# A quarter of a layer's value projection moved into later blocks, a zero fill issued one stage earlier, and idle matmuls in the norm stages

## What is computed

```python
x = x + tanh(g_xattn[0]) * L0_xattn(layernorm(x), ctx, ctx, ...)   # 8x8 heads of width 2
x = x + tanh(g_ffn[0])   * L0_ffn(layernorm(x), ...)               # top-2 of 8 experts, capacity 256
x = x + tanh(g_xattn[1]) * L1_xattn(layernorm(x), ctx, ctx, ...)   # 16 heads of width 64
x = x + tanh(g_ffn[1])   * L1_ffn(layernorm(x), ...)               # int8 matmul
x = x + tanh(g_xattn[2]) * L2_xattn(...)                           # 16 heads of width 8, biased
x = x + tanh(g_ffn[2])   * L2_ffn(...)                             # dense mix of 15 experts
x = x + tanh(g_xattn[3]) * L3_xattn(...)                           # 16 heads of width 8, masked
x = x + tanh(g_ffn[3])   * L3_ffn(...)                             # ternary weights
```

## Time and profile before

| | us |
|---|---|
| median of three runs | 1626.92 |
| the profiled execution, its own time | 1622.71 |
| span of its trace | 1620.9 |
| PE busy | 1379.8 (85%) |
| DVE busy | 1062.6 (66%) |
| ACT busy | 778.8 (48%) |
| POOL busy | 649.0 (40%) |
| mean granted clock of TensorE | 0.895 of 2.4 GHz |

### The profile page before, as it was taken

How to read it: one execution, slowest core, us unless ns; L and a number is a source line. 1 busy time by engine, 2 the same in 40 slices (tenths; PEclk the granted TensorE clock), 3 DMA queues, 4 the chain that set the end, 5 groups by cost and what they waited for, 6 DMA issues and landing times. The chain is left out here.

```text
span 1620.9 us, 29634 instructions
## 1 busy us (share of the span) xinstructions
PE 1379.8 (85%) x10158; PEld 739.9 (46%) x10166; DVE 1062.6 (66%) x3273; ACT 778.8 (48%) x1105; POOL 649.0 (40%) x505
## 2 busy tenths in 40 slices
PE   5999965749999999998339999997999489999981
PEld 3444453615666666666313333333677223333431
DVE  4887744166676666764688777763556787777725
ACT  3777721336665665654113555554433125555550
POOL 4666613514676666777632112200600432332000
PEclk7999976958999999999557999998899769999995
DMA  4566623535342233400054334401200133223001
GB/s 140 193 238 233 241 88 118 157 123 214 143 151 90 101 143 145 155 1 1 17 118 78 75 73 110 86 2 45 48 1 1 25 49 54 38 42 59 13 2 29
DMA packets 87990, 147.57 MB, mean 91 GB/s; under 512 B 15875, under 2 KB 61086, under 8 KB 84261
## 3 DMA queue, kind: packets, MB, share of 16 engines
q1 hardware_dynamic: 84510, 116.94, 25.9%
q10 hardware_dynamic: 1824, 25.17, 4.0%
q0 software_dynamic: 1520, 3.68, 0.9%
HBM read 93.66 MB, written 45.11 MB: 86 GB/s over the span
## 5 line engine op out<-in xcount | busy, mean ns | idle before, releaser
L1834 DVE CUSTOM_DVE_ANT_0 a_junk<-a_psM,a_madd 128x512 bf16<-128x512 f32 x512 | 332.2, 683 | 92.1 <-issue 89.4
L1780 ACT ACTIVATE a_probs<-a_psE 128x1024 f32<-128x1024 f32 x256 | 262.0, 1023 | 214.8 <-PE a_psE L1669 213.9
L2235 DVE TENSOR_REDUCE a_mx<-a_psM 128x1 f32<-128x512 f32 x236 | 148.1, 668 | 124.2 <-PE a_psM L2060 124.2
L1669 PE MATMUL a_psE<-a_maddT,res_identb 64*128 64x512 bf16 x1024 | 221.8, 388 | 2.1
L1646 PE MATMUL a_psM<-narrow_k_op,narrow_q_op 57*128 57x512 bf16 (+1 forms) x512 | 153.0, 415 | 42.1 <-DMA narrow_q_op<-a_y_parts 20.3
L2197 ACT ACTIVATE a_probs<-a_psE 128x1024 f32<-128x1024 f32 x128 | 130.8, 1024 | 85.3 <-PE a_psE L2082 82.0
L190 POOL TENSOR_SCALAR res_xn<-res_X,res_mv,n_rstd 128x128 f32<-128x128 f32 x32 | 26.8, 847 | 352.9 <-DVE n_rstd L176 352.9
L1680 PE MATMUL a_psO<-a_probs,narrow_values 128*32 128x256 f32 x2048 | 164.0, 394 | 2.5 <-ACT a_probs L1780 1.1
L2030 POOL TENSOR_TENSOR a_half_sum<-a_probs 128x1024 f32<-128x1024 f32 x64 | 150.8, 2356 | 32.9 <-ACT a_probs L2197 32.7
L2078 PE MATMUL a_psE<-a_qT,a_kT 64*128 64x256 f32 x1024 | 133.4, 380 | 0.0
L2094 PE MATMUL a_psO<-a_probs,a_values 128*64 128x256 f32 x1024 | 124.6, 385 | 0.8 <-ACT a_o_raw L2181 0.8
(11 more groups left out here) (334 smaller groups left out, 2528.4 us busy)
## 6 DMA issues: line engine op xcount, KB each, us to landing
wide_k<-a_k_stage SPq DMA_DIRECT2D x32, 512.0 KB, 3.2
wide_v<-a_v_stage SPq DMA_DIRECT2D x32, 512.0 KB, 4.3
a_k_part<-wide_k SPq DMA_DIRECT2D x64, 256.0 KB, 3.4
a_kT<-wide_k ACTq DMA_DIRECT2D x6, 2048.0 KB, 8.2
a_values<-wide_v ACTq DMA_DIRECT2D x6, 2048.0 KB, 8.6
keys<-a_parts SPq DMA_DIRECT2D x96, 64.0 KB, 2.0
narrow_q_op<-a_y_parts SPq DMA_DIRECT2D x192, 32.0 KB
narrow_k_op<-keys SPq DMA_DIRECT2D x30, 192.0 KB
```

Source lines behind the costliest of these rows:

```text
L1669: return pe.matmul(psE[s % 2][:, j, :, :], res.identb[group, :], maddT[r][group, s % 2 * 2:s % 2 * 2 + 2, :], start=False, stop=last, skip ...
L1780: act.activation(probs[:, head:head + 2, k:k + 2, :], psE[s % 2][:], ACT.Exp).then_inc(exped, 1)
L1834: dve.tensor_tensor_reduce(junk[j][:], psM[j][:], madd[r][:, t, :], 1.0, -3.0e38, ALU.add, ALU.max, mx[r][:, max_place(h, t):max_place(h, ...
L2235: dve.tensor_reduce(mx[r][:, at:at + 1], max_bank(2 * p + t, j, first), AX.X, ALU.max).then_inc(max_read, 1)
```

## The change

1. `v_stage`, the stores and the loop of wide values in the first layer's attention go from four key tiles to three (KT - 1). The fourth tile's two matmuls per chunk are made by a new class `LateValues`: chunks 0 to 3 in the router's block (`queue_up`), chunks 4 to 7 in the experts' block. `w1v` and `ctxT` stay in SBUF until then. Each chunk has a stage buffer of its own; two PSUM banks are shared.
2. The zero fill of `y_dram` is issued in `project_out`, from a tile cleared by DVE, and its end is awaited there.
3. `norm_phase`, where transposed, starts its PE program with 36 matmuls of bf16 128x128 by 128x128 into a bank that nobody reads.

```diff
+IDLE_MATMULS = 36
+def keep_busy(pe, res, bank, n):
+    for _ in range(n):
+        pe.matmul(bank, res.identb[:], res.onesb[:], start=True, stop=True)
@@ norm_phase
             def _(pe):
                 if transposed:
+                    keep_busy(pe, res, psI[:], IDLE_MATMULS)
                     for c in range(NCHUNK):
@@ attend_layer0
-        n_wide = W_PAIRS + KT * VC
+        n_wide = W_PAIRS + (KT - 1) * VC
...
-                    for k in range(KT):
+                    for k in range(KT - 1):
                         sp.wait_ge(wide_out, n_wide * n + W_PAIRS + VC * (k + 1))
                         sp.dma_start(res.wide_v[one, :, k].rearrange("o p c -> (o p) c"), v_stage[k][:]).then_inc(wv_stored[k], 16)
...
-                    for k in range(2, KT):
+                    for k in range(2, KT - 1):
                         wide_values(i, k, first)
@@ project_out
+    zeros = ph.sb("zeros", [P, 2 * D])
...
-            sp.wait_ge(zeroed, 1)
+            sp.wait_ge(zeroed, 2)
             sp.dma_start(bo[0:1, :], io[bo_name].unsqueeze(0)).then_inc(w_in, 16)
             for sem, count in res.stores:
                 sp.wait_ge(sem, count * (B * S2 // CHUNK))
+            sp.dma_start(res.y_dram[0:2 * NTILE * P].rearrange("(p n k) d -> p n (k d)", p=P, k=2),
+                         zeros[:].unsqueeze(1).to_broadcast([P, NTILE, 2 * D])).then_inc(y_zeroed, 16)
             constants.sync(sp, io, constants_in)
+            sp.wait_ge(y_zeroed, 16)
...
+            dve.memset(zeros[:], 0.0).then_inc(zeroed, 1)
             dve.memset(bo[:], 0.0).then_inc(zeroed, 1)
@@ new class
+class LateValues:
+    def __init__(self, ph, res, chunks, banks=None):
+        self.stage = [ph.sb(f"late{j}", [P, WIDE_V]) for j in range(len(chunks))]
+        self.ps = banks or [ph.ps(f"psV{i}", [P, CHUNK]) for i in range(2)]
+    def tensor(self, pe):
+        for j, n in enumerate(self.chunks):
+            keys = self.res.ctxT[:, 2 * n:2 * n + 2].rearrange("d t n c -> d (t n c)")[:, (KT - 1) * P:KT * P]
+            for c in range(VC):
+                m = VC * j + c
+                if m >= 2:
+                    pe.wait_ge(self.out, m - 1)
+                pe.matmul(self.ps[m % 2][:], keys, self.res.w1v[:, c * CHUNK:(c + 1) * CHUNK], start=True, stop=True).then_inc(self.made, 1)
+    def scalar(self, act):
+                act.wait_ge(self.made, m + 1)
+                act.copy(self.stage[j][:, c * CHUNK:(c + 1) * CHUNK], self.ps[m % 2][:]).then_inc(self.out, 1)
+    def sync(self, sp):
+        for j, n in enumerate(self.chunks):
+            sp.wait_ge(self.out, VC * (j + 1))
+            sp.dma_start(self.res.wide_v[n, :, KT - 1], self.stage[j][:]).then_inc(self.stored, 16)
+    def finish(self, sp):
+        sp.wait_ge(self.stored, 16 * len(self.chunks))
@@ queue_up
+    late = LateValues(ph, res, range(B // 2))
             sp.dma_start(xn_dram.rearrange("(t p) d -> p t d", p=P), res.xn[:]).then_inc(xn_out, 16)
-            sp.wait_ge(zero_made, 1)
-            sp.dma_start(y_dram[0:2 * N_TOKENS]..., zeros...).then_inc(y_zeroed, 16)
+            late.sync(sp)
             sp.wait_ge(xn_out, 16)
-            sp.wait_ge(y_zeroed, 16)
+            late.finish(sp)
...
             router.scalar(act)
+            late.scalar(act)
             act.wait_ge(router.hot, 2)
             act.copy(chose[:], onehot[:]).then_inc(ones_cast, 1)
...
+            late.tensor(pe)
             pe.wait_ge(ones_cast, 2)
...
-            pool.memset(zeros[:], 0.0).then_inc(zero_made, 1)
@@ queued_experts
+        late = LateValues(ph, res, range(B // 2, B), banks)
                 load(0, 0)
                 load(1, 1)
+                late.sync(sp)
                 for e in range(2, E):
                     sp.wait_ge(made, e - 1)
                     load(e, e % 2)
+                late.finish(sp)
...
+                late.tensor(pe)
                 turn(0)
...
             def _(act):
+                late.scalar(act)
                 for e in range(E):
```

More of the change, by code:

```diff
@@ L160, in norm_phase @@
         psT = [ph.ps(f"psT{i}", [P, CHUNK]) for i in range(2)]
+        psI = ph.ps("psI", [P, P])
         var_done, std_done, newton = ph.sem("var_done"), ph.sem("std_done"), ph.sem("newton")
@@ L271, in attend_layer0 @@
     k_stage = [outer.sb(f"k_stage{i}", [P, 2, S2]) for i in range(4)]
-    v_stage = [outer.sb(f"v_stage{i}", [P, WIDE_V]) for i in range(KT)]
+    v_stage = [outer.sb(f"v_stage{i}", [P, WIDE_V]) for i in range(KT - 1)]
     parts = [outer.sb(f"parts{i}", [P, 3, CHUNK], BF16) for i in range(2)]
@@ L305, in attend_layer0 @@
         wide_made, wide_out = ph.sem("wide_made"), ph.sem("wide_out")
-        wk_stored, wv_stored = [ph.sem(f"wk_stored{i}") for i in range(4)], [ph.sem(f"wv_stored{i}") for i in range(KT)]
+        wk_stored, wv_stored = [ph.sem(f"wk_stored{i}") for i in range(4)], [ph.sem(f"wv_stored{i}") for i in range(KT - 1)]
         minus_done = ph.sem("minus_done")
@@ L778, in vector @@
         dve.wait_ge(self.hot, top_k)
+class LateValues:
+    def __init__(self, ph, res, chunks, banks=None):
+        self.res, self.chunks = res, chunks
+        self.stage = [ph.sb(f"late{j}", [P, WIDE_V]) for j in range(len(chunks))]
+        self.ps = banks or [ph.ps(f"psV{i}", [P, CHUNK]) for i in range(2)]
+        self.made, self.out, self.stored = ph.sem("late_made"), ph.sem("late_out"), ph.sem("late_stored")
+    def tensor(self, pe):
[7 more added lines that the diff above has]
+    def scalar(self, act):
+        for j in range(len(self.chunks)):
+            for c in range(VC):
+                m = VC * j + c
+                act.wait_ge(self.made, m + 1)
[6 more added lines that the diff above has]
+        sp.wait_ge(self.stored, 16 * len(self.chunks))
 def layer0_experts(nc, io, res):
@@ L975, in queued_experts @@
         psH = [ph.ps(f"psH{i}", [P, C]) for i in range(4)]
-        psY = [ph.ps(f"psY{i}", [P, ROW_HALVES, D]) for i in range(2)]
+        banks = [ph.ps(f"psY{i}", [P, CHUNK]) for i in range(2)]
+        psY = [bank[:, 0:ROW_HALVES * D].rearrange("p (r d) -> p r d", d=D) for bank in banks]
         w_in, x_in = [ph.sem(f"w_in{i}") for i in range(2)], [ph.sem(f"x_in{e}") for e in range(E)]
@@ L1040, in _ @@
                         pe.matmul(psH[k][:], w1[b][:, k * P:(k + 1) * P], xgT[b][:], start=True, stop=True).then_inc(hidden, 1)
+                    if e == 0:
+                        pe.wait_ge(late.out, VC * len(late.chunks))
                     if e >= 2:
@@ L1080, in _ @@
                     dve.wait_ge(made, e + 1)
-                    dve.tensor_copy(y[:, e], psY[e % 2][:]).then_inc(y_copied, 1)
+                    dve.tensor_copy(y[:, e], psY[e % 2]).then_inc(y_copied, 1)
                 for c in range(NCHUNK):
@@ L2566, in build @@
                 layer0_attention(nc, io, res)
-            Phase.clear_used(nc)
-            layer0_experts(nc, io, res)
+                Phase.clear_used(nc)
+                layer0_experts(nc, io, res)
             norm_phase(nc, io, res, "n2")
```

14 lines of the change are left out of this document (6 added, 8 removed).

## The result

The changed kernel takes 1600.67 us (median of four runs, 1599.92 to 1602.52) against 1626.84 us before (four runs, 1626.61 to 1629.39): ratio 0.9838, 95% interval 0.9824 to 0.9851. That is 26.2 us less, where the prediction had 13.4 less and a range that ended at 1606.0. The sign was right; time and range were wrong. The profiled execution took 1600.32 us for a span of 1598.6; its mean granted clock is 0.915 of full speed against 0.895 before.

What follows compares the result with a forecast made beforehand. PE was taken to bound the first layer's attention. Terms -13.3 + 2.5 + 1.3 + 0 + 0.7 - 0.6 - 4.0 = -13.4 us took the median 1626.92 to 1613.5 us, range 1606 to 1620.5.

Steps and rivals of the forecast that it cites:

- Part 1a: First layer's attention: two of 16 wide value matmuls leave each chunk, and project_out starts earlier; -13.3 us.
- Parts 1b and 1c: Late value matmuls of four chunks each: +2.5 us in the router's block, +1.3 us in the experts' block.
- Part 2: Zero fill moved from the router's block to project_out, covered there by DVE's work: 0 (to +1) us.
- Part 3: 36 idle matmuls per norm: late first transposes +0.7 us; raised clock -0.6 in n0, n2, n6 and -4.0 in n1, n5.
- The rivals: No clock gain in n1 and n5, 0.20; late matmuls stay cold, 0.04; norms overrun, 0.05; POOL takes over attention, 0.06.
- The slower one: In the norms, idle matmuls pay their weight loads in full and overrun: +23 against -9.5, 1640 us; chance 0.05.

Runs made afterwards that it cites:

- e13: The kernel before, unedited, profiled again on one more chip for its experts' loop: 1628.16 us.
- e12: The changed kernel with the zero fill issued in the router's block again: 1603.39 us, ratio 0.9866 to the kernel before.
- e1: The changed kernel without its idle matmuls, 0 instead of 36: 1615.07 us, ratio 0.9947 to the kernel before.
- e2: The kernel before with only the idle matmuls of the six norms added: 1613.65 us, ratio 0.9924.
- e11: The changed kernel with 18 idle matmuls per norm instead of 36: 1614.82 us, ratio 0.9923 to the kernel before.
- e14: The kernel before, unedited, a second time on the same one more chip: 1626.80 us.
- e8: The changed kernel with both first transposes and 14 idle matmuls ahead of the bias row's wait in the first layer's output projection: 1598.13 us, ratio 0.9852.
- e15: The changed kernel, without further edit, on the same chip as two repeats of the kernel before: 1605.35 us.
- e6: The kernel before, unedited, profiled once more as the yardstick: 1620.02 us.

## Why the prediction was wrong

**Part 1a** was right: from the first exponential to the output projection it is 177.3 us before in three profiles and 175.5 in e13, where the clock happened to rise earlier, and 162.1 in all four of the changed kernel. With the clock alike, 175.5 - 162.1 = 13.4 us, against 13.3.

**Parts 1b and 1c** were right: +2.6 against +2.5, +1.1 against +1.3. The late matmuls took 8.99 and 9.57 us (9.6 predicted), and the first gathered turn came 258.33 - 248.93 = 9.4 us after the block's start. In the router's block the clock took another way than mine: still full at the start, 0.50 from 226.5 to 229.5, full from 230 on. I had it low for the first 5 us, and the cold share came out much alike, which is partly luck. Both terms lay in the lower half of wide bounds. One bound was mis-added: with all eight matmuls cold the cast comes at 246.6 + 14.5 + 0.7 = 261.8, which is +7.8 and not +6.9.

**Part 2** was right at 0, as far as e12 can tell. project_out does not end on SP either: DVE's idle time ahead of n1's variance is 1.46 us in both kernels.

**Part 3** is the step that failed, in size: -3.9 us predicted, -8 to -13 measured (e1, e2, e11). Three sentences of it failed.
- "but the work there left the clock at 0.50 for ten microseconds before, so the clock will probably fall again." So I took 2.0 us each in n1 and n5. In the changed kernel the clock was at 1.00 through transposes and logits. Work that doesn't raise a low clock by itself did run on at the full one: n1 took the whole bound, 4.5 us, and n5 3.8. I had weighed a row at the low level as if it said what happens from the high one.
- "In n0, n2 and n6 DVE sets the pace of the transposes and only the last four gain". That DVE sets the pace held (PE waits 0.20 to 0.34 us for scaled tiles between n6's transposes), n6 itself gained 0.5 to 0.6 us in place of 0.2, and the sentence was too narrow. A warm clock is handed on to the next block: in n6 it is the query projection, 5.65 to 3.92 us. In interval A the start of the attention gained 1.9 us beyond the 13.4 of part 1a, because the clock rose earlier there. Some 1.3 of them lie between the first two exponentials: 12.8 to 12.9 us in three profiles of before, 11.0 in all four of the changed kernel, but also in e13 and in e1, which have no idle matmuls. The rest lies between n0's last transpose and the first exponential: 18.0 to 18.2 us before, 16.8 and 16.9 in two profiles of the changed kernel and 18.2 in the other two, and 16.93 in e1. So no run shows that these 1.9 us belong to the idle matmuls; how much of them does stays open.
- "In n4 the gap is 2.66 and they are 1.2 late, of which a warm PE regains half: **+0.7**." The transposes come 0.8 to 1.1 us later, near what I worked out, but a warm PE regained more than all of it: the next block's projection starts 6.97 to 7.37 us after n4's variance, where all four profiles of before have 7.54 or 7.55. The term was -0.4 in place of +0.7. The other half of G's -0.9 is no gain of the change: in e13 and e14 the clock was low in that projection (5.24 and 5.34 us in place of 3.77).

My lower end, 1606, let n1 and n5 run warm throughout and the late matmuls cost half (which sums to -20.3, not to the -21 that I wrote). The gain in n4 and in the starts of the blocks behind the other norms was in no bound. By the intervals the whole is -23.2, below that end; of the three timed comparisons the second, -17.7, would have lain inside my range.

**The rivals.** None came true. The slower one, weight loads that aren't hidden, falls with the row at 215.32: 36 pairs in 3.40 us, 0.094 us each, and at most 0.111 (4.00 us in n5), against the 0.15 from which it would decide. The Trainium skill's rule that I had weighed there ("TensorE: Matmul & The Clock Gate", "Part 3: Packing small matmuls — row/col tiling", overlap only where the row group differs) doesn't describe these loads, and the measurement decides.

**The yardstick.** The profiled execution of before, at 1622.71, lay 4.2 us under its median. On a chip with the stall in E the same kernel took 1626.80 and 1628.16, without it about 1620. I had shifted the sum to the median as it stood, which is right, but I had read interval E's 35.6 us as a constant of the kernel.

## What to carry over

If PE stands idle ahead of a chain that runs at the half clock, fill the whole gap with matmuls on data at hand: 36 that reached up to within 0.6 us of n1's transposes gave 8 to 13 us over six norms, 18 gave none. Price such a warm-up by all the work up to where the trace shows the clock fall again, in the next block too, and read the clock at both levels before calling a stretch cold by nature. An edit that warms one stretch can leave the next one cold (e8), so measure each placement as a whole, and take a difference of a few us between single profiles as shown only if it repeats.

## What the runs showed of the hardware

- The clock that a piece of work gets depends on what ran before it: e8 and the changed kernel have the same instructions in n1, and interval B is 14.41 us in the one and 10.2 to 10.3 in the other's four profiles. The gain can also come in part: with 36 idle matmuls n5's interval H was 11.4 to 11.5 us in e2, e8 and e15 and 10.1 to 10.5 elsewhere, against 14.4 without.
- Interval E runs from 35.6 to 44.4 us over all profiles: on one of the four later chips 35.6 to 37.7, on the other three 40.7 or more, whichever version ran there.
- Other stretches repeat closely: from the first exponential to the output projection it was 162.10 to 162.13 us in eleven of the twelve profiles whose attention had part 1a, so small changes there can be read from single profiles. The twelfth, e1, had 162.93.
- f32 transposes do run at the full clock, and they can raise it: eight in 1.47 us in the changed n1, of which the first are at 219.03, against 1.96 in the earlier trace rows. The Trainium skill, "TensorE: Matmul & The Clock Gate", section "Part 4: PE-mode transpose", says that the full clock doesn't engage in transpose mode. By these rows it does for the transposes of this kernel (`pe.transpose`; the profile shows one record each and doesn't name the mode).

In n0 of the kernel before, sixteen transposes are PE's first work of the whole program. From the view of their tile, eight at the start and four at the end, with the shortest, median and longest duration in ns:

```profile
L218 PE MATMUL n_psT<-res_ident,res_xn x8: 421/421/470, 15.0 to 16.5; 128*128 128x128 f32 x8
...
L218 PE MATMUL n_psT<-res_ident,res_xn x4: 272/276/385, 17.6 to 18.1; 128*128 128x128 f32 x4
```

The step from 421 to 272 ns is that from the low level of the clock to the full one, with nothing but transposes before it; e6 and e14 show it too. In e13 all sixteen took 421 ns or more, and the matmuls behind them, from 20 us on, ran at 1.00.
